# Order of steps in a four-layer graph network: splits put one by one among the T steps, normalisation pieces and weight sums put behind other steps

## The reference, cut to what matters

```python
# layer 0: per-node weights w[n] = sum_d embedding[n, d] * weight[d], K = 3
As = [eye, adj, 2 * (adj @ adj) - eye]
x = layernorm(x + einsum('bnki,nkio->bno', stack(A @ x for A in As), w) + b)
# layer 1: twice z = relu((adj @ z) @ W_i)
x = layernorm(x + z)
# layer 2
x = layernorm(x + x @ W_self + (adj @ x) @ W_neighbor + bias)
# layer 3: x_cat = [x, A x, 2 A A x - x, A x, 2 A A x - x], both supports are adj
x = layernorm(x + x_cat @ weight + bias)
```

## Time and profile before

| | us |
|---|---|
| median of 3 runs (1260.17 to 1260.38) | 1260.37 |
| profiled execution, its own time | 1260.20 |
| span of its records | 1258.2 |
| TensorE busy in the span | 1228.9 |
| VectorE busy in the span | 758.8 |
| ScalarE busy in the span | 215.5 |

### The profile page before, as it was taken

The page is one execution under the profiler, slowest core; times in us unless marked ns, Lnnn a source line. Parts: engine busy times, 40 slices in busy tenths (PEclk is TensorE's granted clock), DMA queues, the critical chain, the costliest instruction groups (busy, mean ns, idle before and its releaser), DMA issues.

```text
span 1258.2 us, 16358 instructions
## 1 busy us (share of the span) xinstructions
PE 1228.9 (98%) x5872; PEld 1028.3 (82%) x5872; DVE 758.8 (60%) x1863; ACT 215.5 (17%) x392; POOL 62.0 (5%) x52
## 2 busy tenths in 40 slices
PE   8999999999999999999999999999999999999996
PEld 6888888788878887878888888878888888888875
DVE  5836897787776777778635554462246255544624
ACT  5622111121111101120111111020111111110110
POOL 0000000000000000000000001010000000010100
PEclk9999999999999999999999999999999999999998
DMA  9832112211111110101011032033001111320320
GB/s 342 327 101 60 38 49 65 72 45 39 52 55 55 47 38 24 44 22 43 15 34 34 20 90 64 13 105 80 1 27 42 34 34 28 86 64 9 95 58 36
DMA packets 128646, 78.16 MB, mean 62 GB/s; under 512 B 97312, under 2 KB 108064, under 8 KB 126752
## 3 DMA queue, kind: packets, MB, share of 16 engines
q1 hardware_dynamic: 128560, 77.05, 21.1%
HBM read 53.42 MB, written 23.59 MB: 61 GB/s over the span
## 4 chain that ended last, share of the span: by engine, by line
PE 90%; DVE 6%; DMA 2%; issue 1%; SPq 1%; ACT 1%; DVEq 0%; ACTq 0%
PE ps L672 29%; PE ps L673 29%; PE ps L776 20%; PE ps L690 8%; PE ps L711 2%; PE ps L712 2%; DVE nat L1038 1%; DVE ring L1038 1%; DMA raw<-in_at 1%; PE ps L684 1%; DVE xs L936 1%; DVE sml L980 0%; SPq L1080 0%; ACT xs L810 0%; DVE sml L971 0%
## 5 line engine op out<-in xcount | busy, mean ns | idle before, releaser
L672 PE MATMUL ps<-B,xs 128*128 128x512 f32 x1664 | 654.9, 394 | 4.2 <-DVE xs L936 4.2
L673 PE MATMUL ps<-B,xs 128*128 128x512 f32 x1664 | 648.0, 389 | 0.0
L672 PEld LDWEIGHTS ps<-B,xs 128*128 128x128 f32 x1664 | 312.6, 188 | 67.9 <-ACT xs L810 3.9
L673 PEld LDWEIGHTS ps<-B,xs 128*128 128x128 f32 x1664 | 312.7, 188 | 62.3
L776 PE MATMUL ps<-Tw,xs 128*128 128x512 f32 x1280 | 309.3, 391 | 2.5 <-DVE ring L1038 2.5
L776 PEld LDWEIGHTS ps<-Tw,xs 128*128 128x128 f32 x1280 | 238.6, 188 | 55.1 <-DVE ring L1038 4.6
L924 DVE TENSOR_TENSOR ring<-ps,rrep 128x512 f32<-128x512 f32 x94 | 64.5, 689 | 252.7 <-PE ps L673 244.2
L1038 DVE SCALAR_TENSOR_TENSOR nat<-ps,embn,nat 128x128 f32<-128x128 f32 x448 | 153.6, 343 | 51.1 <-PE ps L776 50.8
L1038 DVE SCALAR_TENSOR_TENSOR ring<-ps,embn,ring 128x128 f32<-128x128 f32 x512 | 175.0, 342 | 0.0
L690 PEld LDWEIGHTS ps<-W,ring 128*128 128x128 f32 x896 | 111.5, 191 | 12.0 <-DVE ring L924 3.7
L690 PE MATMUL ps<-W,ring 128*128 128x128 f32 x896 | 113.2, 275 | 4.4 <-DVE ring L924 2.5
(11 more groups left out here) (66 smaller groups left out, 542.9 us busy)
## 6 DMA issues: line engine op xcount, KB each, us to landing
raw<-in_at SPq DMA_DIRECT2D x13, 1024.0 KB, 16.2
td<-ring SPq DMA_DIRECT2D x32, 256.0 KB, 2.0
ring<-td SPq DMA_DIRECT2D x128, 64.0 KB, 2.5
ring<-in_xn SPq DMA_DIRECT2D x16, 256.0 KB, 2.9
ring_x<-in_xt SPq DMA_DIRECT2D x32, 128.0 KB, 3.2
ring_x<-y1d SPq DMA_DIRECT2D x32, 128.0 KB, 3.2
out<-nat SPq DMA_DIRECT2D x16, 256.0 KB, 2.3
y1d<-ring SPq DMA_DIRECT2D x14, 256.0 KB, 2.8
```

The source lines that it names most:

```text
L672: pe.matmul(bank, x[:, 0, m, :], of, start=m == 0, stop=False)
L673: mm = pe.matmul(bank, x[:, 1, m, :], of, start=False, stop=ends and m == NT - 1)
```

## The change

Only `order()` and the name of one step change; every instruction of the kernel stays, and no instruction is added.

- In `closing`, the step `split(j + 2, 0, 3)` now stands before `deviate(j, 1, 3)` instead of behind it.
- In `per_node`, the four steps join, centre, deviate and normed now stand behind the `yield`, and so behind the quarters that `weave` puts in after a T step.
- `split_ahead` goes. For pass 1 of chunks 2 and 3 and pass 3 of chunk 2 (`ahead`), split 0 now stands at the end of the pass before, ahead of its last `after`; split 1 stands between two T steps; splits 2 and 3 stand behind the quarters 0 and 1 of the pass's first product. The reload of chunk 2 follows the split 3 of pass 3.
- Weave 3 has lead 3 instead of 2: its 22 quarters begin a T step later and lie closer together.
- The sums of the weights are a step of their own, `sums`, in front of the splits of pass 4 of chunk 2; the transfer of the weights stays at step `W`.

```diff
--- before.py
+++ after.py
@@ -45,6 +45,10 @@

     def put(kind, *at):
         steps.append(Step(kind, *at))
+
+    def ahead(j, p):
+
+        return p == 1 and j > 1 or (j, p) == (2, 3)

     def one_pass(j, p):

@@ -88,6 +92,10 @@
             if p == 5 and c > 0 and m == 1:
                 put("back", j, p, c - 1, 1)
             put("mm", j, p, c, m)
+            if ahead(j, p) and (c, m) in ((0, 0), (0, 1)):
+                put("split", j, p, m + 2)
+            if (j, p, c, m) == (2, 3, 0, 1):
+                put("reload", j)
             if c > 0 and p >= 2 and m == (3 if c == 1 and order[2] == (1, 0) else 0):
                 finish(c - 1)
             if m < 3:
@@ -103,6 +111,8 @@
                 put("normed", j, p, 2)
                 exchange(2)
             yield True
+        if ahead(j, p + 1):
+            put("split", j, p + 1, 0)
         put("after", j, p, 3)
         if norm:
             put("centre", j, p, 3)
@@ -126,9 +136,9 @@
         if i == 1:
             put("centre", j, 1, 3)
         if i == 2:
-            put("deviate", j, 1, 3)
             if j < 2:
                 put("split", j + 2, 0, 3)
+            put("deviate", j, 1, 3)
         if i == 3:
             put("normed", j, 1, 3)
             if j < 3:
@@ -154,8 +164,6 @@
                     put("prep", j, (u + 1) % 2, (u + 1) // 2)
                 if j > 0 and u == 0:
                     closing(j - 1, e)
-                if c > 0 and half == 0:
-                    put(("join", "centre", "deviate", "normed")[e], j, min(e, 1), c - 1)
                 if c < 3 and half == 1 and e == 1:
                     put("prep2", j, 0, c + 1)
                 if j < 3 and c > 0 and half == 1 and e == 3:
@@ -167,21 +175,18 @@
                 if u == 7 and j < 2 and e == 1:
                     put("part", j + 2, 0, 2)
                 yield
+                if c > 0 and half == 0:
+                    put(("join", "centre", "deviate", "normed")[e], j, min(e, 1), c - 1)

     def splits(j, p):
         for c in range(NC):
             put("split", j, p, c)

-    def split_ahead(j, p):
-
-        for c in range(NC):
-            put("split", j, p, c)
-            if c % 2:
-                yield None
-
     def layer0(j):
         yield from one_pass(j, 0)
-        yield from split_ahead(j, 1)
+        yield None
+        put("split", j, 1, 1)
+        yield None
         yield from one_pass(j, 1)

     def head():
@@ -231,9 +236,9 @@

     def layer1(j):
         yield from one_pass(j, 2)
-        yield from split_ahead(j, 3)
-        if j == 2:
-            put("reload", j)
+        yield None
+        put("split", j, 3, 1)
+        yield None
         yield from one_pass(j, 3)

     def weave(j, products, quarters, lead, tail, coming):
@@ -261,6 +266,8 @@
                 yield
         for p in (4, 5, 6):
             yield
+            if (j, p) == (2, 4):
+                put("sums")
             splits(j, p)
             yield
             for whole in one_pass(j, p):
@@ -313,7 +320,7 @@
     products, coming = coming, layer1(2)
     weave(2, products, 30, 2, 2, coming)
     products = coming
-    weave(3, products, 22, 2, 0, None)
+    weave(3, products, 22, 3, 0, None)
     closing(3, 0)
     put("W")
     lanes = [lane0(products), lane1()]
@@ -1038,7 +1045,7 @@
                             dv.scalar_tensor_tensor(sums[d % 2], ps[:, 4 + 2 * p:6 + 2 * p, i * C:(i + 1) * C],
                                                     embn[:, t, d:d + 1], first[d] if d < 2 else sums[d % 2],
                                                     ALU.mult, ALU.add).then_inc(s_acc, 1)
-                    if s.kind == "W":
+                    if s.kind == "sums":
                         dv.wait_ge(s_w, 48)
                         dv.tensor_tensor(W[:, 4, :], W[:, 4, :], W[:, 6, :], ALU.add).then_inc(s_w0, 1)
                         dv.tensor_tensor(W[:, 3, :], W[:, 3, :], W[:, 5, :], ALU.add).then_inc(s_w0, 1)
```

## The result

The changed kernel takes 1253.65 us (median of 5 runs, 1252.46 to 1256.36) against 1260.38 (5 runs, 1260.17 to 1261.65): a ratio of 0.9941, 95% interval 0.993 to 0.9953. The forecast was 1254.4 with a range of 1252.4 to 1257.5. The profiled execution is the slowest of the five, 1256.36 us; what it shows beyond the change is told at the end.

A forecast was written before the change was run, and what follows sets the result against it. TensorE bounds the kernel, busy 1228.9 of 1258.2 us, so only its waits can be won. The terms sum to -6.25, taken as -6.0: 1260.2 gives 1254.2, the median 0.17 higher, 1254.4 us; range 1252.4 to 1257.5.

The forecast's parts named there:

- D: Weave 3, scale before centre and splits of (2,3) spread out: 0.95 us gained at the weighing, 1.6 at a T step.
- E: Reload behind the last split of weave 3: later fetches delay VectorE's prep, 0.55 us lost in two near misses.
- G: Normalisation pieces behind a step's quarters: they swap with an equally long scale or nothing, no gain; bounds 1.0 lost, 0.3 gained.
- A: Weaves 1 and 2, fourth split before the deviation: TensorE's wait for that split goes, 2.0 us gained.
- B: Pass 1 of chunks 2 and 3, splits a quarter ahead: VectorE's T work ends sooner, 0.5 us gained twice, 1.0 together.
- C: Start of weave 3, lead 3: a 1.45 us wait goes, new ones of 0.95 and 0.55 come, sum about 0.
- F: Weight sums moved later: VectorE no longer waits for W, so TensorE's wait on a scale behind it goes, 1.25 us gained.
- the first: Rival: weave 3's gains are lost to new waits in T steps back to back, 1256.1 or 1257.4 us; chance 0.23.
- the second: Rival: every wait named goes and none comes, 8.9 us gained, 1251.5 us; chance 0.08.
- the third: Rival: VectorE is the bound and each wait moves to its next T step, nothing gained, 1260.4 us; chance 0.09.
- fourth: Rival: fetches behind the reload land late, VectorE's prep(3,1,3) holds up TensorE, 1262.9 us or more; chance 0.05.
- the lower figure that was weighed: The Trainium skill's spacing of 512-column matmuls on TensorE, about 131 ns: a quarter of 1.05 us, sum near nothing.

The follow-up runs named there:

- e1: Kernel before the change with one edit, the fourth split put before the deviation in closing: 1257.92 us in one run, against 1260.21.
- e4: Changed kernel with lead 2 instead of 3 in weave 3: 1252.76 us.
- e3: Changed kernel with the splits of pass 3 of chunk 2, and the reload behind them, put back as before: 1253.42 us.
- e9: Kernel before the change with one edit, join, centre, deviate and normed put behind the quarters of their T step: 1260.90 us in one run.
- e10: Kernel before the change with one edit, lead 3 in weave 3: 1260.78 us.
- e7: Changed kernel with the reload put one quarter later, behind the two fetches that stood behind it in SyncE's queue: 1253.91 us.
- e5: Changed kernel with the four sums of the weights put back at step W: 1253.87 us.
- e6: Changed kernel with join, centre, deviate and normed put back before the quarters of their T step: 1253.66 us.
- e12: Changed kernel with spill behind fetch, chunk 3's first weighing of pass 5 a quarter later, chunk 1's pass 6 splits spread: 1251.49 us median, ratio 0.9922.
- e8: Changed kernel with the first weighing of pass 5 put one quarter later: 1251.67 us.
- e2: Changed kernel with the splits of pass 1 of chunks 2 and 3 put back in two pairs: 1256.05 us.
- e11: Changed kernel with the spill of a chunk's last piece put behind the next prep's fetch in SyncE's queue: 1253.94 us in one run.

## Why the prediction was right, and where a step of it was wrong

The time, 1253.65, lies 0.75 us from the forecast and in its own range of 1253.2 to 1255.6. Its main mechanism held: TensorE's waits were local, each went when its own cause went, and VectorE was not the bound. In weave 3 the sum is near by luck, since the errors of D, E and G cancel. By the parts, with the sums worked out from the table:

- **A**, forecast 2.0: measured 2.08 (1.03 and 1.04, and e1 alone). The step held as written: the cast moves to the place behind the square, and nothing behind it becomes late.
- **B**, forecast 1.0: measured 1.2. I had kept 0.1 us in each weave for a wait that would be covered with nothing to spare; it is covered.
- **C**, forecast 0: measured -0.10, which is within what traces differ by, with the two new waits of 0.70 and 0.33 us where the prediction put them. e4 shows the trade.
- **D and E**, forecast 0.95 + 1.6 - 0.55 = 2.0: measured 2.60. The step that failed is "because VectorE stood 1.48 us for ScalarE and then did two splits at 560.10 ahead of its T work", with "After the change one split stands there, already cast" as the cure: the whole 1.6 us is put down to the place of the splits. The splits' place gives 0.62 (e3). The pieces behind the quarters give 1.60 alone (e9), 0.65 more than the 0.95 of the weighing, because the deviation's root no longer holds up the eviction and the casts on ScalarE. I had read the idle time of 1.48 us in the earlier trace rows and not asked what ScalarE was doing in it. The lead gives the last 0.4 (e10).
- The **reload** was charged 0.55 and costs nothing (e7). The idle time itself was forecast right, 2 to 3 us.
- **F**, forecast 1.25: 1.22 by e5. The sums at 632.98 are hidden.
- **G**, forecast 0: nothing in weaves 1 and 2, by e6 and e9. In weave 3 "they swap with a scale of the same length or with nothing" is wrong: the deviation there also swaps with an eviction and two casts on ScalarE, as said under D.

Together 7.1 us against 6.0 to 6.25. The rivals: the first (weave 3 gives back what it gains) is wrong, the second too, since C's waits came; the third and fourth are out, and e7 shows that even the wait of VectorE, from which the fourth starts, costs TensorE nothing. The matmul spacing is 0.227 us after the change too (36 of them from 821.76 to 829.92 us), so the lower figure that was weighed has no part in this kernel.

One sign of being wrong did show: the stretch behind the weaves is not of the same length as before, but 2.1 us longer in the profile. It is not the order that made it so: e7, with the same order there, is within 0.04 us of the kernel before. The last section says where the 2.1 us lie.

## What to carry to other kernels

In a queue that runs in order, ask of each late instruction what stands ahead of it on its own engine, and what that one waits for: a root that waited for VectorE stood on ScalarE ahead of an eviction and casts that could have run, and moving it behind them gave more for one wait than spreading out the splits. When an engine idles for another, read the queue of that other engine too. Short waits at distant places add up to within 0.1 us when each is cured by its own cause (A, B and F); two cures of the same wait overlap, and what is gained ahead of a wait that ends on a transfer can be lost there (1.2 of 1.7 us in e12). Compare two traces step by step from a common start: effects of over 0.2 us can be read there in one run each, where the total time of a run moves by 2 us or more.

## What was not expected

The granted clock of TensorE fell to half, 1.2 GHz, for a short stretch in the changed kernel's profile. Windows of that trace (length, busy us of each engine with its instructions, then the granted clock, DMA share, GB/s):

```profile
831.00:835.00 4.00, 2.02 (x10) 1.37 (x10) 3.20 (x7) 0.60 (x1) 0.00 (x0) 1.00 0.59 130
836.00:839.00 3.00, 3.00 (x14) 2.81 (x14) 1.37 (x3) 0.72 (x2) 0.00 (x0) 0.50 0.44 70
839.00:843.00 4.00, 4.00 (x19) 3.31 (x18) 0.60 (x1) 0.00 (x0) 1.29 (x1) 1.00 0.70 198
```

The timeline of TensorE in the half-clock stretch:

```profile
837.91 0.77 PE L679 MATMUL ps<-B,xs 128*128 128x512 f32 x1
838.48 0.63 PE L680 MATMUL ps<-B,xs 128*128 128x512 f32 x1
```

Just before, TensorE had waited 1.99 us for the transfer. These two matmuls start 0.57 us apart in place of 0.23. Across this place the changed kernel's lead over the kernel before falls from 7.07 to 5.27 us; the wait itself is 0.2 longer, and the rest, about 1.6, is put down to the clock. The other 0.26 us go near 1180, at the second wait on a transfer. Of the other kernels that keep this wait, at 1.8 to 2.2 us, none shows half clock there, so the wait alone doesn't bring it; e8 and e12, without the wait, don't show it either. What decides stays open. (All fourteen profiles also show half clock over their last 9 to 12 us, behind the last matmul, where it costs nothing.)

The head of the kernel, which no edit touches, varies more than most of the edits are worth. In five of the fourteen profiles (the change, e2, e7, e9, e11) the records show half clock once near 24 us; their first T step starts at 113.83 to 114.11 us, in the other nine at 111.75 to 113.27. The profiled execution of the change has both and is the slowest of its five runs. The other four have no records of instructions, but their mean granted clock is known: 0.994 in the two slowest (1256.36 and 1256.19 us), 0.996 in the three others (1252.46 to 1253.65), which fits.
